# Routing tables inside the shared experts' last group, one program part for the feed-forward layer, and softmax by halves in cross-attention

## The reference

```python
x = x + attn(layernorm(x))                # squared-relu attention against 512-channel weights
x = x + xattn(layernorm(x), ctx, mask)    # 16 heads of 64, 128 keys, softmax
x = x + ffn(layernorm(x))

def ffn(x):
    shared = silu(x @ sg) * (x @ su) @ sd             # 512 -> 1024 -> 512
    logits = x @ gate_w                               # 32 experts
    ids, score = argmax(logits), sigmoid(max(logits))
    order = argsort(ids)
    s = (x * score)[order]                            # grouped by expert
    routed = (silu(s @ rg[e]) * (s @ ru[e])) @ rd[e]  # e: the expert of the row
    return shared + routed[argsort(order)]
```

## Time and profile before

| | |
|---|---|
| time, median of 3 runs | 3037.04 us (3036.64 to 3038.77) |
| the profiled execution: time | 3048.35 us |
| its span, first to last instruction | 3046.2 us |
| TensorE busy | 2851.5 us, 94% |
| VectorE, ScalarE, GpSimd busy | 1790.8, 1601.6, 1054.5 us |
| mean granted TensorE clock | 0.968 |

### The profile page before, as it was taken

The page is one execution under the profiler, slowest core; times in us unless marked ns, Lnnn a source line. Parts: engine busy times, 40 slices in busy tenths (PEclk is TensorE's granted clock), DMA queues, the critical chain, the costliest instruction groups (busy, mean ns, idle before and its releaser), DMA issues. The chain is left out here.

```text
span 3046.2 us, 45896 instructions
## 1 busy us (share of the span) xinstructions
PE 2851.5 (94%) x13284; PEld 2309.1 (76%) x13285; DVE 1790.8 (59%) x2648; ACT 1601.6 (53%) x2755; POOL 1054.5 (35%) x637
## 2 busy tenths in 40 slices
PE   7999999999589999999869999999399999999998
PEld 5888888888477777777757888878288888888886
DVE  6566666564565555556453333333777774766776
ACT  6888887887354544455421111111266653654665
POOL 5888888888311111111100000000133332333333
PEclk9999999999799999999979999999699999999999
DMA  1000000000401111111041111111588883767775
GB/s 59 25 25 18 19 24 28 24 10 13 155 21 42 41 34 49 42 32 32 30 136 53 58 55 55 55 65 52 194 282 295 296 296 131 277 233 243 275 276 184
DMA packets 185541, 322.69 MB, mean 106 GB/s; under 512 B 23656, under 2 KB 42088, under 8 KB 185472
## 3 DMA queue, kind: packets, MB, share of 16 engines
q1 hardware_dynamic: 173680, 295.56, 28.4%
q0 software_dynamic: 11792, 26.25, 2.5%
HBM read 286.86 MB, written 46.66 MB: 109 GB/s over the span
## 5 line engine op out<-in xcount | busy, mean ns | idle before, releaser
L156 POOL TENSOR_TENSOR a_pL<-a_p,a_pH 128x1024 fp32r<-128x1024 f32 x256 | 615.2, 2405 | 150.7 <-DVE a_p L344 149.1
L344 DVE TENSOR_TENSOR a_p<-a_r,a_pS 128x1024 f32<-128x1024 f32 x256 | 312.4, 1220 | 282.0 <-ACT a_r L163 275.7
L1440 DVE TENSOR_TENSOR e_wL<-e_raw,e_wH 128x1024 fp32r<-128x1024 f32 x384 | 449.8, 1216 | 32.0 <-ACT e_wH L1435 29.1
L1435 ACT CAST e_wH<-e_raw 128x1024 fp32r<-128x1024 f32 x384 | 385.1, 1053 | 120.3 <-PE d_pD L49 64.2
L732 POOL TENSOR_TENSOR b_S<-b_S,b_ri 128x1024 f32<-128x1024 f32 x64 | 121.4, 1897 | 569.4 <-DVE b_ri L829 569.4
L163 ACT ACTIVATE a_r<-a_pS 128x1024 f32<-128x1024 f32 x256 | 261.9, 1023 | 100.0 <-PE a_pS L49 95.3
L163 ACT ACTIVATE a_pH<-a_r 128x1024 fp32r<-128x1024 f32 x256 | 272.0, 1062 | 9.0
L1515 POOL DMA_INDIRECT out<-d_og,d_iw x46 | 124.0, 2696 | 360.9 <-DVE d_og L1636 360.9
L1308 POOL MEMSET r_ones<- 128x128 bf16 x1 | 0.2, 205 | 607.8 <-POOLq L997 607.8
L47 PE MATMUL a_pS<-a_qH,a_kH 128*128 (+1 forms) x512 | 206.0, 402 | 0.6 <-DVE a_p L344 0.6
L47 PE MATMUL a_pO<-a_pH,a_vH 128*128 128x512 f32 x512 | 201.9, 394 | 0.6 <-POOL a_pL L156 0.6
(11 more groups left out here) (299 smaller groups left out, 7221.9 us busy)
## 6 DMA issues: line engine op xcount, KB each, us to landing
e_raw<-in_L_ffn_routed_gate_w SPq DMA_DIRECT2D x256, 256.0 KB, 4.3
e_raw<-in_L_ffn_routed_up_w SPq DMA_DIRECT2D x256, 256.0 KB, 5.4
e_raw<-in_L_ffn_routed_down_w SPq DMA_DIRECT2D x128, 512.0 KB, 6.3
a_xb<-in_x SPq DMA_DIRECT2D x8, 1024.0 KB, 5.7
x<-a_o SPq DMA_DIRECT2D x32, 256.0 KB, 2.3
b_xb<-x SPq DMA_DIRECT2D x32, 256.0 KB, 2.8
b_xr<-x SPq DMA_DIRECT2D x32, 256.0 KB, 3.1
x<-b_xr SPq DMA_DIRECT2D x32, 256.0 KB, 2.5
```

The lines of the kernel that those rows point to most:

```text
L156: nc.gpsimd.tensor_tensor(pL[:, j % RING, :, :], p[:, j % 2, :, :], pH[:, j % RING, :, :].bitcast(F32), ALU.subtract).then_inc(s["low"], 1)
L344: v.tensor_tensor(p[:, j % 2, :, :], r[:, j % 2, :, :], pS[j % 2][:, :, :], ALU.mult).then_inc(s["p"], 1)
L1435: copy(self.wH[:, n, :, :], self.raw[:, n, :, :]).then_inc(self.s["high"], 1)
L1440: unit.tensor_tensor(self.wL[:, n, :, :], self.raw[:, n, :, :], self.wH[:, n, :, :].bitcast(self.F32), self.sub).then_inc(self.s["low"], 1)
```

## The change

`shared_experts`, `routing_tables` and `routed_experts` become one function `feed_forward` with one program part; the buffers of the three stages lie at fixed places over each other.

- `route` also keeps the running sum of the one-hot rows over tiles (`before`), four small additions a group. The counts, the ranks and the first position of each expert come from matmuls on it in the last group (`expert_counts` after step 2, `token_ranks` in step 3). VectorE's rest of the tables is cut into pieces that stand in steps 2 to 7 of the last group and behind the first two output additions. The 32 index matmuls stand between the first and the second down projection.
- `scale` writes the scaled tokens over the normed ones (no `xo`), in step 5 in the last group; normalising for the next group waits for their store.
- SyncE loads four pieces of expert 0 once the last hidden product has ended, three more behind each store. ScalarE makes four high parts, the other eight after all down projections; VectorE makes low parts 0 to 2 between the last output additions, the rest after them.
- The first slot's tokens are gathered as soon as the index is there, and transposed ahead of the last down projection. The expert-change loads start after SyncE's last store.
- In cross-attention the exponentials, `inverse` and GpSimd's product go by halves (4 of the 8 sub-tiles), `t_high` after the fourth exponential instead of the second; `p_transpose` waits for each half. `norm` moves a pair earlier. At a group's end `p_transpose(6)` goes ahead of the next query, and `values(6)` ahead of the next group's scores.

```diff
 # cross_attention: GpSimd
-                        pool.wait_ge(s["rinv"], n + 1)
-                        nc.gpsimd.tensor_tensor(S[:, j % 2, :, :], S[:, j % 2, :, :],
-                                                ri[:, j % 2, :].unsqueeze(2).to_broadcast([P, SUB, KEYS]), ALU.mult).then_inc(s["prob"], 1)
+                        for half in range(2):
+                            at = (slice(None), j % 2, slice(half * HALF, (half + 1) * HALF))
+                            pool.wait_ge(s["rinv"], 2 * n + half + 1)
+                            nc.gpsimd.tensor_tensor(S[at], S[at], ri[at].unsqueeze(2).to_broadcast([P, HALF, KEYS]), ALU.mult).then_inc(s["prob"], 1)
 # ScalarE
+                        exps(n, j, 0)
+                        if j or not first:
+                            t_high(n - 1)
+                        exps(n, j, 1)
                         if j == NPAIR - 1 and not last:
                             q_high(n + 1, 0)
-                        exps(n, j, 0, EARLY)
-                        if j or not first:
-                            t_high(n - 1)
-                        exps(n, j, EARLY, SUB)
 # VectorE
-                            for i in {NPAIR - 4: (0, 1), NPAIR - 2: (2, 3)}.get(j, ()):
+                            for i in {NPAIR - 5: (0, 1), NPAIR - 3: (2, 3)}.get(j, ()):
                                 norm(g + 1, i)
 # TensorE
+                        if j == 0 and not first:
+                            values(n - 2, pb, NPAIR - 2)
                         scores(n, j)
...
+                        if j or not first:
+                            p_transpose(n - 1, (j - 1) % NPAIR)
                         if j == NPAIR - 1 and not last:
                             pe.wait_ge(s["xL"], turn + GT)
                             query(n + 1, 0)
-                        if j or not first:
-                            p_transpose(n - 1, (j - 1) % NPAIR)
 # feed_forward: VectorE in the last group
+                    if last and i == 4:
+                        row_and_slot()
+                    if last and i == 5:
+                        rows(1)
+                    if last and i == 6:
+                        rows(2)
+                    if last and i == 7:
+                        slot_of(0)
...
+                    if last and i == 2:
+                        expert_blocks()
+                    if last and i == 3:
+                        positions()
+                    if last and i == 4:
+                        rows(0)
+                    if last and i == 5:
+                        scale(g)
+                    if last and i == 6:
+                        rows(3)
+                    if last and i == 7:
+                        slot_of(1)
+                        lane_and_tile()
...
                     v.tensor_tensor(o3[:, i % 2, :], pD[i % 2][:, :], xr[:, i % 2, :], ALU.add).then_inc(s["sum"], 1)
+                    if last and i == 0:
+                        expert_of(0, NSLOT // 2 + 1)
+                        indices()
+                    if last and i == 1:
+                        expert_of(NSLOT // 2 + 1, NSLOT + 1)
+                        slot_table()
...
+                        weights.low(dve, v, 0, 0)
+                        weights.low(dve, v, 0, 1)
+                    if last and i == 2:
+                        weights.low(dve, v, 0, 2)
+                        slot_x_low(0)
 # TensorE in the last group
+                    if last and i == 3:
+                        token_ranks()
                     hidden(pU[i % 2][:, :], wuH, wuL, i, s["up"])
...
+                    if last and i == 2:
+                        expert_counts()
...
+                    if last and i == GT - 1:
+                        slot_x_transpose(ds["turn"], 16)
...
                     m.then_inc(s["down"], 1)
+                    if last and i == 0:
+                        slot_tokens()
 # ScalarE
+            act.wait_ge(s["up"], IC * GROUPS)
+            for n in range(EARLY):
+                weights.high(act, nc.scalar.copy, 0, n)
+            slot_x_high(0)
+            act.wait_ge(s["down"], TILES)
+            for n in range(EARLY, PIECES):
+                weights.high(act, nc.scalar.copy, 0, n)
 # SyncE
+                    if last and i == 1:
+                        sp.wait_ge(s["up"], IC * GROUPS)
+                        for n in range(EARLY):
+                            weights.load(sp, 0, n)
                     if i:
                         store(t - 1, i - 1)
+                    if last and i:
+                        for n in range(EARLY + 3 * (i - 1), min(EARLY + 3 * i, PIECES)):
+                            weights.load(sp, 0, n)
```

More of the change, by code:

```diff
@@ L1018, in shared_experts @@
         pL = pX[0:2 * EXP, :, :].rearrange("p a c -> p (a c)")
+        p_count, p_end = p_n[0:EXP, 0, :], p_n[:, 1, 0:EXP]
         s = {n: ctx.enter_context(nc.semaphore("c_" + n)) for n in
-             ("ramp g_in rH rL x_in0 x_in1 r_in0 r_in1 normed xt xH xL gate up sig gated h hH hL logit_ps lt logit top own score xs xs_out"
+             ("const g_in rH rL x_in0 x_in1 r_in0 r_in1 normed xt xH xL gate up sig gated h hH hL logit_ps lt logit top own score xs xs_out"
               " down sum out0 out1").split()}
+        rs = {n: ctx.enter_context(nc.semaphore("r_" + n)) for n in
+              "step counted blocks ranked placed indexed index table".split()}
@@ L1022, in shared_experts @@
+        ds = {n: ctx.enter_context(nc.semaphore("d_" + n)) for n in
+              "zero ix ib iw x_in b_in turn xt xH xL silu h ht hH hL used sum".split()}
         SL = 16
-        RL = 5
+        RL = 5 + GT
+        RAMPS, CONSTS = 3, 9
         parts = []
@@ L1090, in _, with shared @@
             high_parts(act, KC, 2 * KC)
-            def body(g, first, last):
+            def shared(g, first, last):
                 for i in range(IC):
@@ L1167, in _, with shared @@
             low_parts(dve, KC, 2 * KC)
-            def body(g, first, last):
+            dve.wait_ge(s["const"], CONSTS)
+            def shared(g, first, last):
                 for i in range(IC):
@@ new lines, in _, with body, low, gate @@
+            groups(dve, shared)
+            for n in range(3, PIECES):
+                weights.low(dve, v, 0, n)
+            def body(t, e, split):
+                def low(*pieces):
+                    for n in pieces:
+                        if split:
+                            dve.wait_ge(ds["used"], after(t, n))
+                            weights.low(dve, v, e + 1, n)
+                def gate(n):
+                    dve.wait_ge(ds["silu"], 2 * t + n + 1)
+                    dve.wait_ge(ds["h"], 2 * t + 2)
+                    v.tensor_tensor(d_h[:, n, :], d_sg[:, n, :], d_pU[n][:, :], ALU.mult).then_inc(ds["h"], 1)
+                def h_low(n):
+                    dve.wait_ge(ds["hH"], 2 * t + n + 1)
+                    sub(d_hL[:, 4 * n:4 * n + 4, :], pT[n][:, :, :], d_hH[:, 4 * n:4 * n + 4, :]).then_inc(ds["hL"], 1)
+                low(0, 1)
+                gate(0)
+                low(2)
+                h_low(0)
+                low(3)
+                gate(1)
+                slot_x_low(t + 1)
+                low(4, 5)
+                h_low(1)
+                low(6, 7, 8, 9)
+                dve.wait_ge(ds["used"], PIECES * (t + 1) + len(AHEAD))
+                dve.wait_ge(ds["b_in"], 16 * t + 16)
+                dve.wait_ge(ds["turn"], 16 * t + 16)
+                dve.wait_ge(ds["sum"], t + 1)
+                v.tensor_tensor(og[:, :], d_pD[:, :], bg[:, :], ALU.add).then_inc(ds["sum"], 1)
+                low(10, 11)
@@ L1201, in _ @@
+            slots(dve, body)
         @block.tensor
```

779 lines of the change are left out of this document (367 added, 412 removed).

## The result

The changed kernel takes **2952.16 us** (2951.6 to 2952.8), the one before, on the same chip, 3037.9: a ratio of 0.9713, 95% interval 0.9696 to 0.973. The forecast was 2971 with a range from 2957 to 2998.

The account below looks back on a forecast made before the run. TensorE was taken to set the time everywhere but in the 55 us seam and the waits inside cross-attention. The seam's 44.8 us and cross-attention's 21, together 66, came off the median 3037.04: 2971 us, range 2957 to 2998.

Parts of the forecast that it names:

- The seam: Stretch between the last shared down projection and the first slot matmul, with the slots' cold start: 44.8 us won.
- wait for the index pieces: Last shared group, after the first down projection: TensorE waits 1.2 us for VectorE's last table pieces.
- The gather: Fetch of the first slot's tokens, 9.0 us: just hidden behind TensorE's work, with 1 us to spare.
- The rule of the Trainium skill: Seam: VectorE and GpSimd share an SBUF port, so the gather could end 1 to 3 us later, costing 2 us.
- The first product of the slot: First slot's first gate product: TensorE waits about 4.3 us for expert 0's late weight pieces.
- the cold clock: First slot: the wait on the first gate product may lower TensorE's clock again, costing 2 us.
- The 2.4 us a group: Cross-attention: gain at each of seven group ends with the next group's first pairs, 17 us in all.
- 17 and 2: Cross-attention: 17 us won over seven group ends and 2 us at the stage's end, before the clock.
- the deduction of 3.5: Cross-attention: 3.5 us taken off the gain for semaphore delays hidden in the chain.
- the profiled execution's 11.3 us above the median: Whole kernel: profiled 3048.35 us against median 3037.04; same kind of waits assumed, so 66 us came off the median.
- the 5.5 taken off the median: Cross-attention group ends: half of the 11 us won if the clock stays up at all ends.
- Rival 2: Clock stays up everywhere and the slots don't wait: 51 + 28 us won, 2958 us; chance 0.1.

Follow-up runs that it names:

- f_only: The changed kernel's feed-forward with the cross-attention of the kernel before; 2966.32 us, ratio 0.9768 to the kernel before.
- placed: The kernel before in its old program form, with each shared and routed expert buffer at its address of the changed kernel; 3011.83 us, ratio 0.9913.
- pad2112: The kernel before with the buffers of the shared and routed experts moved together 2112 bytes further per partition; 3038.21 us, ratio 1.0001.
- x_only: The kernel before with the changed cross-attention alone; 3021.19 us, ratio 0.994.

## Why the prediction was wrong, point by point

**The seam: right.** 44.8 us were forecast; f_only less what placement gives is 70.7 - 26.2 = 44.5, and the profiled executions of placed and f_only, which are alike outside the seam, differ by 43.7 in their spans. The terms: ranks and counts 1.8 forecast, 1.9 measured; wait for the index pieces 1.2, measured 1.86; index matmuls 3.2, measured 2.73; transposes 0.4, about 0.35 measured. The gather was hidden: it landed at 2095.84, 2.9 us ahead of the transposes at 2098.77. The rule of the Trainium skill that had been weighed (SBUF — State Buffer, Who interferes with whom) would have made it late by up to 2 us; the trace shows none of that: the index copy took 0.18 us, and from its start to the landing were 6.6 us where 9.0 had been counted. The first product of the slot was to wait 4.3, it waited 3.23; the cold clock was to cost 2 and cost about 1.7 (six matmuls at 0.43 from start to start for 0.227, and the transposes 1.06 for 0.60). What I had not counted was the 1.6 us at the entry to the slot loop. So the sum is as close as it is because its errors cancel: 2.4 us that were not foreseen against 1.9 that were counted and did not come.

**Cross-attention: the mechanism right, the clock wrong.** The 2.4 us a group were measured as forecast: 83.5 to 81.1. The waits left at a group end are those for tL, GpSimd's half and x's low part that were named (0.96, 0.23 and 0.59 us at the first end, for 1.05, 0.5 and 0.85). Over the whole stage the traces of pad2112 and x_only differ by 18.0 us, where 17 and 2 had been counted before the clock and the deduction of 3.5. The step that failed here is the sentence that the profiled execution's 11.3 us above the median are waits of the same kind in both. They were the clock at six group ends. So there were 11 us for the clock to win in the profiled execution and about none in the median one, and the 5.5 taken off the median were not there. 21 us were forecast, 15.9 measured (12 to 24 by the interval).

**The slots and the shared groups: the missing term.** This is the step that failed most: for both the forecast counted nothing, and gave no reason. They gave 26.2 us (25 by the traces), more than the whole of cross-attention, through the addresses in the diff. The change's own text moves every buffer, and I took that as bookkeeping of space. This alone carried the time below the range: 3037 - 44.5 - 15.9 = 2976.6 lies inside it, and 2976.6 - 26.2 = 2950.4, measured 2952.2. Rival 2, the nearest in number (2958), would have had the right time for wrong reasons: its clock gain is not there in the median, and the first slot does wait.

## What to carry to other kernels

Before subtracting a saving from a median, check that the profiled execution is a median one; where it is slower, find out at which places the clock fell, since a saving read there may not exist in the others. Where a change moves buffers, compare the start addresses of each matmul's two operands: here, but for the scores of self-attention, a distance that is a whole number of 256 bytes made a 128x512 matmul 2.5% quicker, and a mere change in the order of allocation, small buffers last, brought 20 us in two stages that are otherwise untouched. And a releaser named by the profile is an inference: making its work earlier and seeing the wait stay is a cheap way to clear it.

## What the hardware showed that was not expected

- At granted clock 1.00 a 128x512 matmul starts 0.226 to 0.229 us after the one before it where the two operands lie a multiple of 256 bytes apart in their partitions, and 0.232 to 0.234 us where they lie 64, 96, 128 or 192 bytes off one. The scores of self-attention are an exception that stays open (0.2315 at a distance of 32768). Moving all buffers together by 2112 or 288 bytes changes nothing.
- The Trainium skill (TensorE: Matmul & The Clock Gate, Wait — 56ns, not 53.3ns?) states 215.7 ns from start to start for a matmul of 512 columns when warm, and names no type. These kernels never reached it; the best was about 226 ns, and the measurement decides for matmuls of this type.
- Executions of the same program lie some 10 us apart. In the profiles of the kernel before and of pad2112, whose cross-attention is the same, the difference is the clock at the group ends: 0.74 over the stretch at six of seven in the one, 0.87 at three in the other. With the changed group end it stayed at 1.00 at every one of the seven.
- The same wait of 3.27 us in the first shared group left the clock up in two profiles (placed, f_only) and let it fall in two others (pad2112, the changed kernel), where the 24 matmuls behind it took 8.2 to 8.3 us for 5.6.
